# Shifted keys go straight into the candidate tile, ScalarE's copy is gone, and the engine orders, lags and PSUM banks are new

## The chip, the cores and the metric

The kernel runs on one core of one Trainium2 chip. The metric is device time in microseconds for one execution. The kernel before took 1073.24 us (median of 3 runs, 1071.86 to 1074.42). A core has five engines that run their own instruction queues side by side and meet through semaphores: TensorE (PE, with PEld for its weight loads), VectorE (DVE), ScalarE (ACT), GpSimd (POOL) and SyncE (SP, which here only issues DMAs). TensorE writes PSUM; DVE and ACT read PSUM and SBUF; POOL works on SBUF alone.

## What the reference computes

A transformer layer on 64 sequences of 64 rows of width 128. Three residual steps, each on a layer norm:

```
x = x + xattn(layernorm(x), context)   # 16 heads of 64, 128 context rows of width 96, softmax
x = x + tree(layernorm(x))             # 16 heads, depth 5: sigmoid paths, causal softmax of path agreement
x = x + experts(layernorm(x))          # product keys: 8 heads, two sets of 32 keys, top 10 of the sums
```

In the expert step each head has two score vectors of 32, s1 and s2. The reference takes the top 10 of each, adds all pairs, takes the top 10 pairs, and weighs the gelu of those pairs' hidden units by the softmax of their sums:

```
v1, i1 = top_k(s1, 10); v2, i2 = top_k(s2, 10)
vals, best = top_k(v1[:, None] + v2[None, :], 10)
h = gelu(x @ w_down[expert_idx]) * softmax(vals);  out = h @ w_up[expert_idx]
```

The kernel never gathers. It computes all 1024 hidden units (pairs of the 32 x 32 keys) for every row, forms all 1024 pair sums per head, and masks those below the cut that the top pairs set.

## The kernel before, in words

The 4096 rows are cut into 32 tiles of 128 rows (two sequences). Each tile goes through some 120 steps with names: x.* and y.* for the cross attention, t.* for the tree, k.* for the keys and their selection, e.* for the experts. Five tables (PE_ORDER, ACT_ORDER, DVE_ORDER, POOL_ORDER, SP_ORDER) hold for each engine the order of its steps in one round, and for each step a lag: in round i the engine does the step for tile i minus lag. So the engines work on several tiles at once, and each engine runs its list strictly in order; a step that waits holds all that stands behind it. A table BANK gives each result of TensorE its place in PSUM: four banks x0, x1, t0, t1 for the attention, tree and keys, and two double banks f0, f1 for the experts. A step that takes a bank waits until the last reader of its earlier content is done.

The steps around the change, for one tile:

- k.turn (PE, L528) transposes the third norm, k.high (ACT, L755) and k.low (DVE, L870) split it into two halves of 16 bits, k.key (PE, L540 and L313 to L315) makes the 512 key scores in bank t0, and e.hid (PE, L313 to L315 into psF) the 1024 hidden units.
- k.top (DVE, L944 and L947): 16 maxima of 8, then every score minus its set's maximum, written back into the same bank. k.split (DVE, L956 and L958): the shifted scores, clamped, as two 16 bit halves in the tile `us`. SP sends `us` through a transposing DMA (k.kturn) for the pair sums e.s0 to e.s7 (PE, L592).
- k.inner (POOL, L1075, L1081) writes 8 candidate sums of inner ranks into the tile `cand` of 72 per head; k.shift (ACT, L761) copies the 64 shifted scores of each head from the bank into the rest of `cand`. k.cand (DVE, L971, L976, L981) finds the best 16 of the 72.
- k.eb (ACT, L768), k.z (DVE, L989, L991) and k.lnz (ACT, L773) make the softmax's normaliser; k.cut (POOL, L1093, L1095) the cut.
- e.x (ACT, L790) exponentiates the pair sums of a head, e.w (DVE, L1002) masks them, e.a (POOL, L1123) adds the heads up. e.gelu (ACT, L780 to L782) is a table load, the gelu of the hidden units and a second table load. e.wturn, e.gate and e.out finish the tile, e.add (DVE, L1020) adds the residual.
- Around them on the same engines: x.turn (PE, L327), x.q0 to x.q3 (PE, L313 to L315 into psXT) with their copies x.w (ACT L625, one on DVE L629), the scores x.s (PE, L379), exponentials x.e (ACT, L700) and reciprocals x.r (DVE, L888), normalisation x.n (POOL, L1063), transposes x.p (PE, L398) with copies x.t (ACT, L625), the mix y.m (PE, L420, L422) with copies y.u (ACT, L625), y.out (PE, L439, L441), y.res (DVE, L899, L851 to L856), t.turn (PE, L450), t.sb (ACT, L710), t.pv (PE, L465 to L467), t.pexp and t.v (ACT, L717, L723).

Of the kernel before, what the change touches and what calls it, by code (L numbers as in the profile page):

```python
# [19 lines left out]
NQ = 2 * FH  # L20
# [9 lines left out]
def build(nc, a):  # L30
# [3 lines left out]
    with ctx:  # L34
# [229 lines left out]
        def _(pe):  # L264
# [54 lines left out]
            def x_turn(t):  # L319
                after(pe, "x.t0", t - 1)  # L320
                at_ends(pe, "x.t0", t - 2)
                at_ends(pe, "x.t0", t - 3)
                at_ends(pe, "x.t0", t - 4)
                at_ends(pe, "x.t0", t - 5)
                at_ends(pe, "x.t0", t - 6)
                pe.wait_ge(s["x.norm"], t + 1)
                done("x.turn", pe.transpose(bank[BANK["x.turn"]][:, 0:128], xn[:, t % 2, :], ident[:]))  # L327
            steps["x.turn"] = x_turn

            def queries(k):  # L330
                def step(t):
                    if k == 0:
                        after(pe, "y.res", t - 1)
                        at_ends(pe, "y.res", t - 2)
                        at_ends(pe, "y.res", t - 3)
                        at_ends(pe, "y.res", t - 4)
                        at_ends(pe, "y.res", t - 5)
                        at_ends(pe, "y.res", t - 6)
                    elif k == 1:
                        after(pe, "y.u3", t - 1)  # L340
                        at_ends(pe, "t.div", t - 2)
                        at_ends(pe, "t.div", t - 3)
                        at_ends(pe, "t.div", t - 4)
                        at_ends(pe, "t.div", t - 5)
                        at_ends(pe, "t.div", t - 6)
                        at_ends(pe, "t.div", t - 7)
                    elif k == 2:
                        pe.wait_ge(s["x.high"], t + 1)
                        pe.wait_ge(s["x.low"], t + 1)
                    elif k == 3:  # L350
                        pe.wait_ge(s["x.w2"], t + 1)
# [10 lines left out]
            def scores(k):  # L362
                def step(t):
                    if k == 0:
                        after(pe, "t.sb", t - 1)
                        at_ends(pe, "x.w1", t)
                    elif k == 1:
                        pe.wait_ge(s["x.w3"], t + 1)
                    elif k == 2:
                        pe.wait_ge(s["x.w0"], t + 1)  # L370
                    elif k == 3:
                        pe.wait_ge(s["x.e2"], t + 1)
# [12 lines left out]
            def probs_turn(k):  # L385
                def step(t):
                    if k == 0:
                        pe.wait_ge(s["y.u1"], t + 1)
                    elif k == 1:
                        pe.wait_ge(s["x.e1"], t + 1)  # L390
                    elif k == 2:
                        after(pe, "t.div", t - 1)
                        at_ends(pe, "x.e0", t)
                    elif k == 3:
                        pe.wait_ge(s["x.t2"], t + 1)
                    pe.wait_ge(s[f"x.n{k}"], t + 1)
                    for i in range(4):
                        mm = pe.transpose(bank[BANK[f"x.p{k}"]][:, i * 128:i * 128 + 128], p[:, k, i, :], ident[:])  # L398
                    done(f"x.p{k}", mm)
                return step  # L400

            def mix(k):
                def step(t):
                    if k == 0:
                        pe.wait_ge(s["y.u2"], t + 1)
                    elif k == 1:
                        pe.wait_ge(s["x.t1"], t + 1)
                    elif k == 2:
                        pe.wait_ge(s["x.e3"], t + 1)
                    elif k == 3:  # L410
                        pe.wait_ge(s["x.t3"], t + 1)
# [19 lines left out]
            def cross_out(t):  # L431
                pe.wait_ge(s["y.u0"], t + 1)
# [49 lines left out]
            def similarity(t):  # L482
                pe.wait_ge(s["t.fsb"], t + 1)
# [12 lines left out]
            def tree_mix(t):  # L496
                pe.wait_ge(s["t.exp"], t + 1)
# [15 lines left out]
            def tree_turn(t):  # L513
                pe.wait_ge(s["t.div"], t + 1)
                pe.wait_ge(s["t.div"], t + 1)
# [3 lines left out]
            def tree_out(t):  # L519
                pe.wait_ge(s["t.csb"], t + 1)  # L520
                pe.wait_ge(s["t.csb"], t + 1)
# [3 lines left out]
            def xn3_turn(t):  # L525
                pe.wait_ge(s["t.res"], t + 1)
# [4 lines left out]
            def key_scores(t):  # L531
                pe.wait_ge(s["k.high"], t + 1)
                pe.wait_ge(s["k.low"], t + 1)
# [10 lines left out]
            def hidden(t):  # L544
                after(pe, "e.w6", t - 1)
                at_ends(pe, "e.w6", t - 2)
                at_ends(pe, "e.w6", t - 3)
                at_ends(pe, "e.w6", t - 4)
                at_ends(pe, "e.w6", t - 5)
                at_ends(pe, "e.w6", t - 6)  # L550
# [11 lines left out]
            def sums(h):  # L562
                def step(t):
                    if h == 0:
                        pe.wait_ge(s["e.w2"], t + 1)
                    elif h == 1:
                        after(pe, "e.add", t - 2)
                        at_ends(pe, "e.w7", t - 1)
                        at_ends(pe, "e.add", t - 3)
                        at_ends(pe, "e.add", t - 4)  # L570
                        at_ends(pe, "e.add", t - 5)
                        at_ends(pe, "e.add", t - 6)
                        at_ends(pe, "e.add", t - 7)
                    elif h == 2:
                        pe.wait_ge(s["e.gelu"], t + 1)
                    elif h == 3:
                        pe.wait_ge(s["e.w1"], t + 1)
                    elif h == 4:
                        pe.wait_ge(s["e.w0"], t + 1)
                    elif h == 5:  # L580
                        after(pe, "e.gate", t - 1)
                        at_ends(pe, "e.w3", t)
                    elif h == 6:
                        pe.wait_ge(s["e.w4"], t + 1)
                    elif h == 7:
                        pe.wait_ge(s["e.w5"], t + 1)
# [12 lines left out]
            def w_turn(t):  # L599
                after(pe, "e.w3", t + 1)  # L600
                at_ends(pe, "e.add", t - 1)
# [7 lines left out]
            def experts_out(t):  # L609
                after(pe, "e.w7", t + 1)  # L610
                at_ends(pe, "e.gate", t)
# [52 lines left out]
        def _(act):  # L664
# [137 lines left out]
        def _(dve):  # L802
# [134 lines left out]
            def tops1(t):  # L937
# [5 lines left out]
                for k in range(NQ):  # L943
# [3 lines left out]
                done("k.top", dve.tensor_tensor(keyed, keyed, top[:, t % 2, :, 0:1].to_broadcast([128, NQ, NSQ]),  # L947
                                                ALU.subtract))
            steps["k.top"] = tops1

            def split(t):
# [3 lines left out]
                uh = bank[BANK["k.key"]].rearrange("p (h i) -> p h i", h=FH)  # L955
# [6 lines left out]
            def candidates(t):  # L962

                dve.wait_ge(s["k.shift"], t + 1)
# [251 lines left out]
```

## Time and profile before

| | |
|---|---|
| median of 3 runs | 1073.24 us (1071.86 to 1074.42) |
| span of the profiled execution (first to last instruction) | 1070.5 us |
| PE busy | 973.2 us, 91% |
| POOL busy | 893.0 us, 83% |
| ACT busy | 874.9 us, 82% |
| DVE busy | 872.4 us, 82% |
| TensorE's granted clock, mean | 0.974 of full |

The page gives one profiled execution; its own time is known as its span, which lies 2.7 us below the median of the timed runs. A busy share is an average over the span and is pulled down by the filling and the draining of the pipeline at its ends. Between them every tile looks alike, so one round can be read for all. A row of the timeline has the start in us, the time taken, the engine, the line, the operation and its tiles, and in square brackets how long the engine stood idle before it and what released it. Rows of the same line that follow each other are merged.

### The profile page before, as it was taken

The page shows a single profiled execution, that of the slowest core. Times are in us where ns is not written, and L with a number is a line of the kernel's source. Part 1 is how long each engine was busy: PE and PEld are TensorE (multiplying, and loading weights), DVE is VectorE, ACT ScalarE, POOL GpSimd, SP SyncE. Part 2 cuts the span into 40 slices and gives each one's busy share as a digit, 9 for nine tenths or more (in the row PEclk, how much of TensorE's full clock was granted, in tenths as well). Part 3 has the DMA queues.
Part 4 walks back from the last instruction along what each step waited for, and adds up shares of the span by engine and source line. Part 5 has one row for each costly group of instructions (what it writes and reads, how often), then busy time and mean ns, then how long its engine had stood idle before and what let it go on. Part 6 is the DMA issues. An engine that isn't in the chain of part 4 may idle for free.

```text
span 1070.5 us, 35810 instructions
## 1 busy us (share of the span) xinstructions
PE 973.2 (91%) x12440; PEld 763.0 (71%) x12440; DVE 872.4 (82%) x2877; ACT 874.9 (82%) x2123; POOL 893.0 (83%) x935
## 2 busy tenths in 40 slices
PE   6798999999999999999999999999999999999865
PEld 6676777777777777777777777777777777777533
DVE  3567888888888888888888888888889888888773
ACT  4668899888888988888898888889888888988752
POOL 1338888988998898889888888988888898888866
PEclk9989999999999999999999999999999999999875
DMA  6010001111110111111011111001111100110000
GB/s 168 14 23 21 18 17 27 24 27 27 23 19 16 27 24 27 27 24 23 11 26 25 27 26 27 21 11 27 25 27 26 28 20 11 27 25 21 13 13 5
DMA packets 70367, 27.25 MB, mean 25 GB/s; under 512 B 47312, under 2 KB 69936, under 8 KB 70192
## 3 DMA queue, kind: packets, MB, share of 16 engines
q1 hardware_dynamic: 69152, 24.58, 10.5%
q8 instruction: 103, 1.69, 0.7%
q14 instruction: 72, 0.59, 0.2%
q10 hardware_dynamic: 1040, 0.39, 0.1%
HBM read 14.47 MB, written 2.10 MB: 15 GB/s over the span
## 4 chain that ended last, share of the span: by engine, by line
DVE 38%; PE 29%; POOL 13%; issue 13%; ACT 6%; DVEq 1%; DMA 0%; POOLq 0%; ACTq 0%; SPq 0%
DVE mw L1002 10%; POOL wsum L1123 7%; PE psXT L398 7%; POOL p L1063 5%; PE psXT L420 5%; DVE cand L976 5%; DVE top L944 5%; PE psF L592 4%; DVE best L971 4%; DVE best L981 3%; ACT ew L790 3%; PE psXT L422 2%; DVE us L956 2%; DVE q L629 2%; DVE negmax L879 2%
## 5 line engine op out<-in xcount | busy, mean ns | idle before, releaser
L1123 POOL TENSOR_TENSOR wsum<-wsum,mw 128x1024 f32<-128x1024 f32 x192 | 452.8, 2359 | 3.1
L1002 DVE SCALAR_TENSOR_TENSOR mw<-psF,cut,ew 128x1024 f32<-128x1024 f32 x256 | 324.5, 1278 | 47.9 <-ACT ew L790 45.2
L790 ACT ACTIVATE ew<-psF,lnz 128x1024 f32<-128x1024 f32 x256 | 285.5, 1128 | 12.4 <-PE psF L592 9.3
L700 ACT ACTIVATE p<-psXT,negmax 128x128 f32<-128x128 f32 x512 | 184.0, 400 | 3.8 <-DVE negmax L879 3.7
L592 PE MATMUL psF<-sel,usT 128*128 128x512 f16 x512 | 158.5, 392 | 30.3 <-DVE mw L1002 27.7
L379 PE MATMUL psXT<-cT,q 96*128 96x128 f32 x1024 | 142.4, 282 | 14.3 <-ACT p L700 11.0
L379 PEld LDWEIGHTS psXT<-cT,q 96*128 96x128 f32 x1024 | 124.2, 191 | 43.6 <-ACT p L700 25.9
L1063 POOL TENSOR_TENSOR p<-p,rrow 128x512 f32<-128x512 f32 x128 | 130.3, 1037 | 25.9 <-DVE rrow L888 25.9
L700 ACT ACTIVATION_READ_ACCUMULATOR p<-psXT,negmax 128x1 f32 x512 | 123.9, 242 | 0.0
L420 PE MATMUL psXT<-pT,c 128*32 128x384 f32 x768 | 110.7, 501 | 2.0 <-ACT pT L625 2.0
L422 PE MATMUL psXT<-pT,c 128*32 128x128 f32 x768 | 108.5, 278 | 0.0
L313 PE MATMUL psXT<-xnT,qk 128*96 128x128 f16 x512 | 92.1, 221 | 2.2 <-DVE xnT L870 1.1
L1123 POOL TENSOR_TENSOR wsum<-mw 128x1024 f32<-128x1024 f32 x32 | 75.3, 2355 | 21.7 <-DVE mw L1002 21.7
L441 PE MATMUL psXT<-vo,uT 128*128 128x128 f32 x768 | 92.6, 277 | 0.0
L1053 POOL TENSOR_SCALAR xn<-x,mv,rstd 128x128 f32<-128x128 f32 x96 | 77.5, 808 | 17.6 <-POOL rstd L1050 17.6
L314 PE MATMUL psXT<-xnT,qk 128*96 128x128 f16 x512 | 91.9, 221 | 0.0
L315 PE MATMUL psXT<-xnT,qk 128*96 128x128 f16 x512 | 91.9, 221 | 0.0
L879 DVE TENSOR_REDUCE negmax<-psXT 128x4 f32<-128x512 f32 x128 | 85.1, 665 | 7.9 <-PE psXT L379 7.9
L441 PEld LDWEIGHTS psXT<-vo,uT 128*128 128x128 f32 x768 | 88.3, 192 | 0.0
L761 ACT ACTIVATE cand<-psXT 128x512 f32<-128x512 f32 x32 | 19.1, 597 | 83.9 <-DVE us L958 83.9
L398 PE MATMUL psXT<-ident,p 128*128 128x128 f32 x512 | 83.3, 286 | 4.2 <-POOL p L1063 0.2
L625 ACT ACTIVATE uT<-psXT 128x384 f32<-128x384 f32 x128 | 63.9, 499 | 20.0 <-PE psXT L422 20.0
(133 smaller groups left out, 2340.5 us busy)
## 6 DMA issues: line engine op xcount, KB each, us to landing
cT<-cT_dram SPq DMA_DIRECT2D x32, 96.0 KB, 2.0
c<-c_dram SPq DMA_DIRECT2D x32, 96.0 KB, 2.1
x<-x_dram SPq DMA_DIRECT2D x32, 64.0 KB, 1.8
xr<-x_dram SPq DMA_DIRECT2D x32, 64.0 KB, 2.0
y_dram<-y SPq DMA_DIRECT2D x32, 64.0 KB, 1.5
wqT<-wqT_dram SPq DMA_DIRECT2D x1, 512.0 KB, 5.1
wo<-wo_dram SPq DMA_DIRECT2D x1, 512.0 KB, 6.3
wdT<-wdT_dram SPq DMA_DIRECT2D x1, 512.0 KB, 3.5
```

Source lines behind the costliest of these rows:

```text
L379: mm = pe.matmul(bank[BANK[f"x.s{k}"]][:, i * M:i * M + M], q[:, b, h:h + 2, :].rearrange("c h q -> c (h q)"), cT[:, t % 2, b, :], start=T ...
L398: mm = pe.transpose(bank[BANK[f"x.p{k}"]][:, i * 128:i * 128 + 128], p[:, k, i, :], ident[:])
L420: pe.matmul(to[32 * j:32 * j + 32], cols, probs[:, :, 0:3, :], start=True, stop=True, tile_position=(0, 32 * j))
L422: mm = pe.matmul(to[96:128, :, j, :], cols, probs[:, :, 3, :], start=True, stop=True, tile_position=(0, 96))
L441: mm = pe.matmul(out, uT[:, i, :, :].rearrange("c b q -> c (b q)"), vo[:, i, :], start=False, stop=(i == XH3 - 1))
L592: mm = pe.matmul(bank[BANK[f"e.s{h}"]][:, j * 512:j * 512 + 512], usT[:, t % 4, h, :], sel[:, j * 512:j * 512 + 512], start=True, stop=True)
L700: ins = act.activation(p[:, k, i, :], bank[BANK[f"x.s{k}"]][:, i * M:i * M + M], ACT.Exp, bias=negmax[:, k, i:i + 1], accum_out=rowsum[:, ...
L790: done(f"e.x{h}", act.activation(ew[:, h % NEW, :], bank[BANK[f"e.s{h}"]], ACT.Exp, bias=lnz[:, t % 4, h:h + 1]))
L879: done(f"x.x{k}", dve.tensor_reduce(negmax[:, k, :], bank[BANK[f"x.s{k}"]].rearrange("p (i m) -> p i m", i=4), AX.X, ALU.max, negate=True))
L1002: done(f"e.w{h}", dve.scalar_tensor_tensor(out=mw[:, h % NMW, :], in0=bank[BANK[f"e.s{h}"]], scalar=cut[:, t % 4, h:h + 1], in1=ew[:, h % ...
L1063: done(f"x.n{k}", pool.tensor_tensor(p[:, k, :, :], p[:, k, :, :], rrow[:, k, :].unsqueeze(2).to_broadcast([128, 4, M]), ALU.mult))
L1123: done(f"e.a{h}", pool.tensor_tensor(wsum[:, t % 2, :], mw[:, 0, :] if h == 1 else wsum[:, t % 2, :], mw[:, h % NMW, :], ALU.add))
```

## The change

1. k.top's subtraction (L947) writes its result into `cand` in SBUF and no longer back into the PSUM bank.
2. k.split reads its input from `cand` and not from the bank.
3. k.shift, ScalarE's copy, is gone. k.cand waits for k.top in its place.
4. Four of the five orders are new, and so are the lags and banks. x.stats and x.norm move one tile ahead. Many waits of TensorE that other waits imply are gone, and those that the new banks ask for are new.

```
-                done("k.top", dve.tensor_tensor(keyed, keyed, top[:, t % 2, :, 0:1].to_broadcast([128, NQ, NSQ]),
-                                                ALU.subtract))
+                shifted = cand[:, t % 2, :, 0:2 * NSQ].rearrange("p h (e i) -> p h e i", e=2)
+                done("k.top", dve.tensor_tensor(shifted, keyed.rearrange("p (h e) i -> p h e i", e=2),
+                                                top[:, t % 2, :, 0:1].rearrange("p (h e) o -> p h e o", e=2)
+                                                .to_broadcast([128, FH, 2, NSQ]), ALU.subtract))
...
-                uh = bank[BANK["k.key"]].rearrange("p (h i) -> p h i", h=FH)
+                uh = cand[:, t % 2, :, 0:2 * NSQ]
...
-            def shifted(t):
-                act.wait_ge(s["k.split"], t + 1)
-                after(act, "k.cand", t - 2)
-                done("k.shift", act.activation(cand[:, t % 2, :, 0:2 * NSQ],
-                                               bank[BANK["k.key"]].rearrange("p (h i) -> p h i", h=FH), ACT.Copy))
-            steps["k.shift"] = shifted
...
-                dve.wait_ge(s["k.shift"], t + 1)
+                dve.wait_ge(s["k.top"], t + 1)
...
 PE_ORDER = {
-    "t.pv": 3, "x.s0": 2, "e.s1": 4, "x.q3": 2, "x.s2": 2, "e.s0": 4, "x.s1": 2, "t.fturn": 3, "e.s3": 4,
+    "e.hid": 4, "x.q1": 2, "e.out": 6, "t.turn": 3, "x.q0": 2, "t.pv": 3, "x.q2": 2, "e.s2": 4, "x.s0": 2,
```

The places where the order moves, as the instructions stand in a row. A lag that grows by one while the step goes from the end of a round to the start of the next changes nothing; what moves is this.

On PE, behind the key scores, before: x.turn (L327), the 24 products of e.hid (psF, first rows shown), then y.out (L439, L441), then x.q1.

```order
L327 MATMUL psXT<-ident,xn 128x128
L313 MATMUL psF<-xn3T,wd 128x128
L314 MATMUL psF<-xn3T,wd 128x128
...
L439 MATMUL psXT<-bias,ones 128x128
L441 MATMUL psXT<-vo,uT 128x128 x12
L313 MATMUL psXT<-xnT,qk 96x128
```

The same place on PE now (pair sums e.s7 at L524, y.out at L397 and L399):

```order
L524 MATMUL psF<-sel,usT 128x512 x2
L397 MATMUL psXT<-bias,ones 128x128
L399 MATMUL psXT<-vo,uT 128x128 x12
L313 MATMUL psF<-xn3T,wd 128x128
L314 MATMUL psF<-xn3T,wd 128x128
...
L313 MATMUL psXT<-xnT,qk 96x128
```

y.out has gone ahead of e.hid; e.s7, which stood ahead of k.key, now stands behind it and y.m0; x.turn has gone ahead of k.key.

On ACT, from the last copies of the mix to the exponentials of the best, before (uT is y.u, cand k.shift, gh the gelu, q x.w, xn2T t.sb, ebest k.eb, psXT L717 t.pexp, v t.v):

```order
L790 ACTIVATE ew<-psF,lnz 128x1024
L625 ACTIVATE uT<-psXT 128x6x64
L692 ACTIVATE xnT<-psXT 128x128
L761 ACTIVATE cand<-psXT 128x8x64
L780 ACT_TABLE_LOAD
L781 ACTIVATE gh<-psF 128x1024
L782 ACT_TABLE_LOAD
L625 ACTIVATE q<-psXT 96x4x2x64 x2
L710 ACTIVATE xn2T<-psXT 128x128
L625 ACTIVATE q<-psXT 96x4x2x64
L768 ACTIVATE ebest<-best 128x80
L717 ACTIVATE psXT<-psXT 128x80
```

The same place on ACT now (uT and q at L557, gh at L706, xn2T L642, v L655, psXT L649, ebest L693):

```order
L557 ACTIVATE uT<-psXT 128x6x64
L715 ACTIVATE ew<-psF,lnz 128x1024
L705 ACT_TABLE_LOAD
L706 ACTIVATE gh<-psF 128x1024
L707 ACT_TABLE_LOAD
L557 ACTIVATE q<-psXT 96x4x2x64
L642 ACTIVATE xn2T<-psXT 128x128
L557 ACTIVATE q<-psXT 96x4x2x64
L655 ACTIVATE v<-psXT 128x16x8
L649 ACTIVATE psXT<-psXT 128x80
L693 ACTIVATE ebest<-best 128x80
L557 ACTIVATE q<-psXT 96x4x2x64
```

The copy into cand is gone, so the gelu has only e.hid to wait for; t.v and t.pexp now stand ahead of k.eb, the last x.w behind it.

On DVE, from the keys' maxima to the candidates, before (L870 is x.low, mw e.w7, x and st to mv y.res):

```order
L944 MAX top<-psXT 128x8 x16
L947 TENSOR_TENSOR psXT<-psXT,top 128x512
L870 TENSOR_TENSOR xnT<-psXT,xnT 128x128
L956 TENSOR_SCALAR us<-psXT 128x8x64
L958 SCALAR_TENSOR_TENSOR us<-psXT,us 128x8x64
L1002 SCALAR_TENSOR_TENSOR mw<-psF,cut,ew 128x1024
L899 TENSOR_TENSOR x<-xr,psXT 128x128
```

The same place on DVE now (x.low at L795, k.top L869 and L873, e.w7 L929, k.split L883 and L885, y.res from L824):

```order
L795 TENSOR_TENSOR xnT<-psXT,xnT 128x128
L869 MAX top<-psXT 128x8 x16
L873 TENSOR_TENSOR cand<-psXT,top 128x8x64
L929 SCALAR_TENSOR_TENSOR mw<-psF,cut,ew 128x1024
L883 TENSOR_SCALAR us<-cand 128x8x64
L885 SCALAR_TENSOR_TENSOR us<-cand,us 128x8x64
L824 TENSOR_TENSOR x<-xr,psXT 128x128
```

x.low has gone ahead of the maxima, e.w7 between the subtraction and the split, and both instructions of the split now read cand in SBUF.

On POOL the order around this place stays k.inner, e.a5, t.norm, e.a6, k.cut; x.norm moves from behind k.norm to behind k.cut, and e.a2 from behind three of the x.n to behind two.

## Rows read from the trace of the kernel before

**Rows 1.** Timeline of SP's queue (start, took): transposing DMA of tiles 1 and 28.

```profile
100.16 1.25 SPq L226 DMA_TRANSPOSE usT<-us  x1
...
939.67 1.48 SPq L226 DMA_TRANSPOSE usT<-us  x1
```

**Rows 2.** Chain that ended last, 500 to 600 us: start, took, engine, tile, line.

```profile
562.21 1.68 DVE top L944 x16
...
573.09 0.28 ACT ebest L768
...
580.28 2.36 POOL wsum L1123
...
585.78 0.63 PE psXT L398 x4
```

**Rows 3.** Timeline of PE, one round (start, took, engine, line, operation).

```profile
561.04 0.38 PE L540 MATMUL psXT<-bias,ones 96*128 96x512 f16 x1
...
562.96 0.22 PE L313 MATMUL psF<-xn3T,wd 128*128 128x128 f16 x1
...
564.30 0.22 PE L439 MATMUL psXT<-bias,ones 96*128 96x128 f16 x1
...
567.09 0.22 PE L313 MATMUL psXT<-xnT,qk 128*96 128x128 f16 x1
...
571.37 0.27 PE L450 MATMUL psXT<-ident,xn 128*128 128x128 f32 x1
572.10 0.20 PE L465 MATMUL psXT<-bias,ones 96*128 96x80 f16 x1 [0.46 <-ACT xn2T L710]
...
572.39 0.43 PE L467 MATMUL psXT<-awv,xn2T 128*128 128x128 f32 x2
...
592.40 0.38 PE L540 MATMUL psXT<-bias,ones 96*128 96x512 f16 x1
```

**Rows 4.** Timeline of ACT, the same round.

```profile
562.95 0.49 ACT L625 ACTIVATE uT<-psXT 128x384 f32<-128x384 f32 x1 [0.50 <-PE psXT L422]
...
566.15 0.60 ACT L761 ACTIVATE cand<-psXT 128x512 f32<-128x512 f32 x1 [2.54 <-DVE us L958]
566.77 1.28 ACT L780 ACT_TABLE_LOAD   x1
...
570.40 1.08 ACT L625 ACTIVATE q<-psXT 96x512 f32<-96x512 f32 x2
571.68 0.28 ACT L710 ACTIVATE xn2T<-psXT 128x128 f32<-128x128 f32 x1 [0.20 <-PE psXT L450]
...
573.27 0.22 ACT L717 ACTIVATE psXT<-psXT 128x80 f32<-128x80 f32 x1
```

**Rows 5.** Timeline of DVE, the same round.

```profile
563.91 0.70 DVE L947 TENSOR_TENSOR psXT<-psXT,top 128x512 f32<-128x512 f32 x1
...
564.71 0.68 DVE L956 TENSOR_SCALAR us<-psXT 128x512 f16<-128x512 f32 x1
...
568.78 1.18 DVE L971 MAX8 best<-cand 128x8 f32<-128x72 f32 x8 [0.41 <-issue]
```

**Rows 6.** Page, costliest groups: busy, mean ns of one, then idle before.

```profile
L1002 DVE SCALAR_TENSOR_TENSOR mw<-psF,cut,ew 128x1024 f32<-128x1024 f32 x256 | 324.5, 1278 | 47.9 <-ACT ew L790 45.2
```

**Rows 7.** Timeline of POOL, the same round.

```profile
565.58 0.32 POOL L1075 TENSOR_TENSOR tops<-top 128x80 f32<-128x80 f32 x1
...
566.54 2.36 POOL L1123 TENSOR_TENSOR wsum<-wsum,mw 128x1024 f32<-128x1024 f32 x1
```

**Rows 8.** Timelines of DVE and POOL in the setup, about 30 us.

```profile
29.77 1.10 DVE L831 CAST wd<-wdT 128x1024 f16<-128x1024 f32 x1
...
29.27 1.04 POOL L1063 TENSOR_TENSOR p<-p,rrow 128x512 f32<-128x512 f32 x1 [5.09 <-DVE rrow L888]
30.27 1.01 POOL L1050 TENSOR_TENSOR rstd<-mv,halfneg 128x1 f32<-128x1 f32 x1
```

**Rows 9.** Line L811: duration ns min/median/max of its two forms.

```profile
L811 DVE CAST bias<-bias x2: 254/338/423, 12.4 to 40.3; 96x208 f16<-96x208 f32 x1, 96x512 f16<-96x512 f32 x1
```

More of the change, by code:

```diff
@@ L331, in step @@
                 def step(t):
[L332 to L351, printed above, removed]
                     if t == 0:
@@ L363, in step @@
                 def step(t):
[L364 to L370, printed above, removed]
+                    if k == 2:
+                        after(pe, "t.path", t - 1)
                     elif k == 3:
-                        pe.wait_ge(s["x.e2"], t + 1)
+                        after(pe, "x.e2", t)
                     pe.wait_ge(s["ld.ct"], 16 * (t + 1))
@@ L386, in step @@
                 def step(t):
[L387 to L393, printed above, removed]
+                    if k == 2:
+                        after(pe, "x.e3", t)
                     elif k == 3:
-                        pe.wait_ge(s["x.t2"], t + 1)
+                        after(pe, "t.res", t - 1)
                     pe.wait_ge(s[f"x.n{k}"], t + 1)
@@ L525, in xn3_turn @@
             def xn3_turn(t):
-                pe.wait_ge(s["t.res"], t + 1)
+                after(pe, "x.t3", t + 1)
                 pe.wait_ge(s["k.norm"], t + 1)
@@ L544, in hidden @@
             def hidden(t):
[L545 to L550, printed above, removed]
                 if t == 0:
@@ L600, in w_turn @@
                 after(pe, "e.w3", t + 1)
-                at_ends(pe, "e.add", t - 1)
+                if t >= NT - 1:
+                    after(pe, "e.add", t - 1)
                 pe.wait_ge(s[f"e.a{FH - 1}"], t + 1)
@@ L1134 @@
 PE_ORDER = {
[3 rows of a table removed]
-    "k.key": 3, "y.m0": 2, "x.turn": 1, "e.hid": 3, "y.out": 2, "x.q1": 1, "e.out": 5, "x.q0": 1, "x.q2": 1,
-    "e.s2": 3, "t.turn": 2,
[5 rows of a table added]
 }
 ACT_ORDER = {
[3 rows of a table removed]
-    2, "x.high": 1, "k.shift": 3, "e.gelu": 3, "x.w1": 1, "x.w0": 1, "t.sb": 2, "x.w2": 1,
[4 rows of a table added]
 }
 DVE_ORDER = {
-    "e.add": 6, "k.z": 4, "t.path": 3, "x.x0": 2, "e.w2": 4, "x.w3": 2, "x.x2": 2, "e.w1": 4, "e.w0": 4, "x.x1":
-    2, "x.r0": 2, "e.w3": 4, "x.r2": 2, "x.r1": 2, "x.x3": 2, "e.gate": 5, "t.div": 3, "e.w4": 4, "x.r3": 2,
-    "t.res": 3, "x.stats": 1, "e.w5": 4, "k.low": 3, "e.w6": 4, "k.top": 3, "x.low": 1, "k.split": 3, "e.w7": 4,
+    "e.add": 6, "k.z": 4, "t.path": 3, "x.x0": 2, "e.w2": 4, "x.w3": 2, "x.x2": 2, "e.w1": 4, "e.w0": 4, "x.x1": 2,
+    "x.r0": 2, "x.x3": 2, "x.r2": 2, "e.w3": 4, "x.r1": 2, "e.gate": 5, "t.div": 3, "e.w4": 4, "x.r3": 2,
+    "t.res": 3, "e.w5": 4, "e.w6": 4, "k.low": 3, "x.stats": 0, "x.low": 1, "k.top": 3, "e.w7": 4, "k.split": 3,
     "y.res": 2, "k.cand": 3,
@@ L1153 @@
 POOL_ORDER = {
-    "k.cut": 4, "t.feat": 3, "e.a7": 5, "e.a1": 4, "x.n0": 2, "x.n2": 2, "x.n1": 2, "e.a2": 4, "x.n3": 2,
-    "k.norm": 3, "x.norm": 1, "e.a3": 4, "e.a4": 4, "k.inner": 3, "e.a5": 4, "t.norm": 2, "e.a6": 4,
+    "t.feat": 3, "e.a7": 5, "e.a1": 4, "x.n2": 2, "x.n1": 2, "e.a2": 4, "x.n0": 2, "x.n3": 2, "k.norm": 3,
+    "e.a3": 4, "e.a4": 4, "k.inner": 3, "e.a5": 4, "t.norm": 2, "e.a6": 4, "k.cut": 3, "x.norm": 0,
 }
```

59 lines of the change are left out of this document (13 added, 46 removed), and 23 rows, old and new, of tables (ACT_ORDER, BANK, PE_ORDER).

## The prediction, as put on record before the run

> **What bounds the kernel now.** I read the queue of SP first, for the length of a round; then the chain of waits in the middle of the span, for what the round consists of; then the timelines of the engines over one round, for each leg of that chain. The transposing DMA comes once per tile, and from tile 1 to tile 28 it takes 939.67 - 100.16 = 839.5 us, 31.09 us per round [rows 1]. So the span is some 31 rounds and two ends, and the question is what a round becomes. In the chain the reader is to see that no single engine is the bound: it passes from DVE's maxima of the keys (562.21) over DVE's candidates to ACT's exponentials of the best (573.09), over DVE's masks to POOL's first head sum (580.28), to PE's transposes (585.78), and along PE to the key scores of the next tile [rows 2]. It is a loop through four engines, closed by one step, k.key, to which all comes back.
>
> I cut the loop at two points: the start of k.key (561.04, and 592.40 a round later [rows 3]) and the start of k.eb on ACT (573.09 [rows 2]). The first leg is 573.09 - 561.04 = 12.05 us, the second 592.40 - 573.09 = 19.31 us; together 31.36, a round that is 0.27 above the mean.
>
> The first leg has two strands beside each other. DVE's: maxima, subtraction, split, mask, y.res, candidates. ACT's: its idle 2.54 us for the split, the copy into cand (566.15), the gelu with its two table loads (566.77 to 570.40), the copies of the queries, t.sb, and then k.eb [rows 4]. Today DVE's strand ends last; ACT's is held back by the same split.
>
> **The change, part by part.**
>
> DVE's strand without its neighbours. The subtraction starts 563.91 - 561.04 = 2.87 after k.key and takes 0.70 [rows 3, 5]. From the split's first instruction to the candidates are 568.78 - 564.71 = 4.07, split, mask and y.res together [rows 5]; the order of these changes, not their content. x.low no longer stands between. The split's first instruction now reads SBUF: no row of before has it in this form; the nearest is the setup's cast from f32 to f16, SBUF to SBUF, 512 wide, 0.423 us [rows 9], against 0.68 from PSUM [rows 5]. I take 0.42, with 0.68 as the upper end, so -0.26. The second keeps two inputs of one element a step: nothing. The subtraction with its output in SBUF: nothing, since its input stays in PSUM. From the candidates' start to k.eb are 573.09 - 568.78 = 4.31. Sum: 2.87 + 0.70 + 4.07 - 0.26 + 4.31 = 11.69, that is 0.36 less than 12.05.
>
> ACT's copy. It takes 0.60 and its removal alone would let the gelu start as soon as the hidden units are there. But e.hid has been moved behind y.out, so this strand is to be summed anew. From k.key to the last copy of the mix, y.u0: 562.95 - 561.04 = 1.91, since y.m0 still follows k.key directly (x.turn moved from behind it to ahead of k.key; e.s7, now between y.m0 and y.out, lies beside y.u0). y.u0 0.49 [rows 4], and 0.14 to PE's start, as from t.sb's end (571.68 + 0.28) to t.pv at 572.10 [rows 3, 4]. y.out 567.09 - 564.30 = 2.79; e.hid 564.30 - 562.96 = 1.34, and 0.20 for the end of its last product and the hand-over to ACT (a product of 0.22 that starts 1.34 / 24 = 0.06 before y.out, and 0.04 as from t.turn's end, 571.37 + 0.27, to t.sb at 571.68) [rows 3, 4]. Here ACT stands idle, longer than the 2.54 of before. The gelu 570.40 - 566.77 = 3.63; one copy of queries, half of 1.08, is 0.54; t.sb 0.28; 0.14 to PE; t.pv 572.39 + 0.43 - 572.10 = 0.72, and 0.04 back; then t.v and t.pexp, which now stand ahead of k.eb, at the 573.27 - 573.09 = 0.18 by which such small instructions follow each other, 0.36 [rows 2 to 4]. Sum: 1.91 + 0.49 + 0.14 + 2.79 + 1.34 + 0.20 + 3.63 + 0.54 + 0.28 + 0.14 + 0.76 + 0.36 = 12.58. So the strand that took the cover of the copy is now the longer one: 0.53 more than 12.05.
>
> The second leg. POOL does the same five steps from e.a1 to the last x.n, with e.a2 one place earlier; the first transposes could start sooner, the third, which waits for the last x.n, not. On PE e.s7 (two products) leaves the stretch from there to k.key and x.turn (one) enters. On ACT, e.x6 now stands ahead of the copy x.t3, on which k.turn now waits for its bank, and y.u2 ahead of k.high; that gives back what PE gains. I cost the leg at 19.31, unchanged, with 0.3 either way. x.norm on POOL, moved behind k.cut, fills POOL's wait for t.path and costs nothing.
>
> The new contact of DVE and POOL. In the setup the only DVE instructions from SBUF to SBUF of the split's kind meet POOL at work. The 1024 wide cast at 29.77 took 1.10 us, where the two widths of L811 (0.254 for 208, 0.423 for 512) lead on to about 0.71; POOL's x.n was under way from 29.27 to 30.31, and the cast ended 0.56 after that, so it lost 0.39 of the 0.54 that they overlapped. POOL's next instruction, one element wide, took 1.01 [rows 8, 9]. So such an instruction waits behind a POOL instruction in flight, and POOL behind it. In a round POOL answers the end of the subtraction by k.inner, 566.54 - 565.58 = 0.96 us, and then the head sum e.a5, 2.36 us [rows 7]. The subtraction ends 2.87 + 0.70 = 3.57 after k.key; k.inner starts about 0.1 later (an estimate, between the hand-overs of 0.04 and 0.14 above), if POOL is idle there, which its shorter round allows; e.a5 runs from 4.63 to 6.99. DVE does the mask first, 1.28 [rows 6], and comes to the split at 4.85, just after e.a5 has started. Held to 6.85 (the cast got on about 0.14 before POOL's recorded end), it loses 2.0 us. If it wins the race instead, its second instruction, with two inputs in SBUF, meets e.a5, with much the same loss. The first leg is then 11.69 + 2.0 = 13.69, 1.64 more than before, and DVE's strand is the longer again. The stall is between nothing, where the two don't block each other, and 2.36, a whole e.a5; I take 2.0, as the one row that shows the case has nearly the full overlap lost.
>
> The Trainium skill ("SBUF — State Buffer", section "Who interferes with whom") says that a DVE instruction in a two-port mode, or with two SBUF inputs beside a GpSimd instruction that reads SBUF, and a GpSimd instruction keep each other out for the whole instruction. The setup's cast agrees but for 0.14; no row shows it for a head sum. By the rule the stall is 2.1 where the sum has 2.0. "VectorE: DVE Perf Modes", section "What auto-detection actually checks", gives such a mode to one-source instructions with both ends in SBUF, which the 0.423 of the cast bears out; the split's first instruction would be one.
>
> **The sum.** A round is 13.69 + 19.31 = 33.00, against the mean of 31.09, so 1.91 more. Of the 31 distances between 32 tiles I count 28, leaving out two while the pipeline fills and one while it drains: 28 x 1.91 = 53.5 us. The profiled span of 1070.5 lies 2.7 below the median of the runs; I add the difference to the median: 1073.2 + 53.5 = 1126.7, so 1127.
>
> **The rivals.**
>
> First: DVE and POOL do not hold each other up, or for less than the 0.9 by which ACT's strand (12.58) exceeds DVE's (11.69). Then the loop runs over y.u0, y.out, e.hid, gelu and t.pv: 12.58 + 19.31 = 31.89, 0.80 above the mean, 28 x 0.80 = 22, so 1096. For it: one short overlap in the setup is all that shows the blocking, and not beside a head sum. Against it: the 1.10 and the 1.01 of that overlap.
>
> Second, on the other side: ACT's strand is shorter than I read, because PE gets to e.hid sooner. If e.hid ends 0.89 earlier than in my sum, and the split is not held, DVE's strand alone counts: 11.69 + 19.31 = 31.00; and the 0.36 by which this leg shrinks would come off the mean round too: 31.09 - 0.36 = 30.73, up to 0.1 less with PE's stretch shorter. 28 x 0.45 = 12.6, so 1061. It decides from the point at which ACT's strand falls below 12.05 - 0.27 = 11.78. For it: PE stands idle in the round (0.46 ahead of t.pv [rows 3]), and e.s7 has moved. Against it: y.out can't start ahead of y.u0, and each term is from a row.
>
> Third: gains and losses cancel, 1073, with ACT's strand near 11.8 and a stall under 0.2.
>
> **How the numbers follow.** A stall that ends last 0.47, ACT's strand 0.26, faster 0.19, no change 0.08. The likeliest gives 1127; with its stall between 1.3 and 2.36 and the second leg 0.3 either way, 28 x (1.2 to 2.3) gives 1107 to 1137 for it alone. The range for 8 in 10 runs from 1062 to 1137: it takes in the stall of nothing (1096), no change, and about half of the faster case. Within 0.2% (2 us) a measurement of this kernel can't tell from no change. Faster 0.19, same 0.08, slower 0.73.
>
> **What would show it.** In the profile of the changed kernel: the transposing DMAs 33.0 apart. The split's first instruction with a recorded time well above 0.42, near 2.4 if its wait is inside, or the second one likewise, each time beside e.a5; or else e.a5 longer than 2.36. k.eb 13.7 after k.key's start, waiting for DVE's candidates. If k.eb is 12.6 after k.key and DVE waits for ACT there, with ACT idle over 3 us for e.hid, the first rival holds. If the split's first instruction takes 0.42 beside e.a5, with k.eb under 11.8 after k.key, I am wrong in both steps. If the second leg is off 19.31 by over 0.5, my reading of PE's and ACT's new order there is wrong.

## The result, and the profile after

The changed kernel took 1128.32 us (median of 4 runs, 1126.6 to 1132.16), the kernel before beside it 1073.5 (1071.86 to 1074.42): ratio 1.0516 [1.0501, 1.0532], slower, 1.3 us above the forecast of 1127. The span of its profiled execution is 1126.8 us, 56.3 more than before. The medians of the kernel before beside the experiments lie between 1072.9 and 1074.4.

SP's queue of the changed kernel gives the length of a round, as [rows 1] did (start, took):

```profile
70.45 1.37 SPq L226 DMA_TRANSPOSE usT<-us  x1
108.96 1.25 SPq L226 DMA_TRANSPOSE usT<-us  x1
...
990.24 1.24 SPq L226 DMA_TRANSPOSE usT<-us  x1
```

The last two are of tiles 1 and 28: 881.28 / 27 = 32.64 us a round, 1.55 more than before; 27 of these are 41.8 us. The other 14.5 are at the ends: the first transpose comes 2.6 later than before (67.81 there), the distance to the second is 38.51 instead of 32.35, and from tile 28 to the end of the span are 136.6 instead of 130.8.

Inside a round, PE's timeline of the changed kernel (start, took, engine, line, operation) to be held against [rows 3]: k.key, y.out, e.hid, the next k.key.

```profile
589.99 0.38 PE L482 MATMUL psXT<-bias,ones 96*128 96x512 f16 x1
...
592.44 0.23 PE L397 MATMUL psXT<-bias,ones 96*128 96x128 f16 x1
...
595.24 0.22 PE L313 MATMUL psF<-xn3T,wd 128*128 128x128 f16 x1
...
622.53 0.38 PE L482 MATMUL psXT<-bias,ones 96*128 96x512 f16 x1
```

ACT's timeline of the same round, for [rows 4], with the idle time ahead in brackets: the last mix copy, the gelu's table load, t.pexp, k.eb.

```profile
591.89 0.49 ACT L557 ACTIVATE uT<-psXT 128x384 f32<-128x384 f32 x1 [1.33 <-PE psXT L381]
...
596.85 1.28 ACT L705 ACT_TABLE_LOAD   x1 [3.35 <-PE psF L315]
...
602.38 0.23 ACT L649 ACTIVATE psXT<-psXT 128x80 f32<-128x80 f32 x1
603.30 0.27 ACT L693 ACTIVATE ebest<-best 128x80 f32<-128x80 f32 x1 [0.69 <-DVE best L908]
```

The first leg is 603.30 - 589.99 = 13.31 us (12.05 in the round of before that was read), the second 622.53 - 603.30 = 19.23 (19.31). All that a round lost lies in the first. By the median over the rounds that start with the k.key of tiles 2 to 26 the two legs are 11.70 and 19.30 in the kernel before, 13.31 and 19.24 now: the round of before that was read is longer than most, and the part on the prediction comes back to it. ScalarE now waits 3.35 for e.hid, its strand is done at 602.61, 12.62 after k.key, and k.eb still stands idle 0.69 for DVE. So DVE ends last, and its timeline, for [rows 5 and 6], shows by what:

```profile
592.85 0.69 DVE L873 TENSOR_TENSOR cand<-psXT,top 128x512 f32<-128x512 f32 x1
593.53 1.28 DVE L929 SCALAR_TENSOR_TENSOR mw<-psF,cut,ew 128x1024 f32<-128x1024 f32 x1
594.73 2.50 DVE L883 TENSOR_SCALAR us<-cand 128x512 f16<-128x512 f32 x1
597.26 0.69 DVE L885 SCALAR_TENSOR_TENSOR us<-cand,us 128x512 f16<-128x512 f32 x1
...
599.00 1.18 DVE L898 MAX8 best<-cand 128x8 f32<-128x72 f32 x8
```

POOL's timeline beside it, for [rows 7]:

```profile
593.61 0.32 POOL L1002 TENSOR_TENSOR tops<-top 128x80 f32<-128x80 f32 x1 [0.59 <-DVE cand L873]
594.01 0.61 POOL L1008 TENSOR_TENSOR cand<-tops 128x32 f32<-128x32 f32 x3
594.58 2.36 POOL L1050 TENSOR_TENSOR wsum<-wsum,mw 128x1024 f32<-128x1024 f32 x1
599.03 0.56 POOL L977 TENSOR_TENSOR rstd<-mv,halfneg 128x1 f32<-128x1 f32 x1 [2.09 <-DVE mv L781]
```

The mask (L929) has its old 1.28. The split's first instruction starts 0.15 after POOL's head sum e.a5 and is recorded as busy for 2.50; e.a5 keeps its 2.36 and pays nothing. Then POOL itself stands idle 2.09, for y.res, which is queued on DVE behind the held split. The groups of the split's two lines (duration in ns, minimum, median, maximum) say that this is the rule and not one round:

```profile
L883 DVE TENSOR_SCALAR us<-cand x32: 426/2490/2574, 69.2 to 1084.8; 128x512 f16<-128x512 f32 x32
...
L885 DVE SCALAR_TENSOR_TENSOR us<-cand,us x32: 691/693/2708, 69.7 to 1087.3; 128x512 f16<-128x512 f32 x32
```

The 426 is tile 0, which comes before any head sum. The 2708 is the last tile, where two head sums follow each other on POOL and the second instruction of the split is held as well as the first.

A held instruction looks like a busy one. The page's first part has DVE busy for 66.7 us more (872.4 before), though its list of work has hardly changed:

```profile
PE 982.7 (87%) x12440; PEld 768.1 (68%) x12440; DVE 939.1 (83%) x2877; ACT 859.7 (76%) x2091; POOL 895.4 (79%) x935
```

The groups by line (busy time, mean ns, idle ahead) put 58 us of these on the split, whose two lines were 21.8 and 22.1 us before:

```profile
L883 DVE TENSOR_SCALAR us<-cand 128x512 f16<-128x512 f32 x32 | 77.8, 2432 | 0.0
...
L885 DVE SCALAR_TENSOR_TENSOR us<-cand,us 128x512 f16<-128x512 f32 x32 | 24.2, 756 | 1.1
```

The pipeline's filling, in the view by stretches (length, busy time of PE, PEld, DVE, ACT, POOL, then PE's granted clock), first the kernel before, from its first transpose to its second:

```profile
67.81:100.16 32.35, 28.33 (x364) 21.49 (x363) 24.37 (x87) 27.25 (x67) 20.87 (x27) 0.95 0.09 21
```

and the same stretch of the changed kernel:

```profile
70.45:108.96 38.51, 33.21 (x404) 26.72 (x402) 27.74 (x88) 27.99 (x66) 23.70 (x30) 0.87 0.07 17
```

While few tiles are under way each wait leaves PE idle, and here its clock was granted at 0.87 where before it had 0.95. This stretch alone cost 6.2 us.

### The profile page after: what moved, and what is told of

Read it like the earlier page. It is cut to its first block, busy times and chain, and to the rows that moved or that the text cites. A ratio compares the mean times of both kernels' runs of the same rounds, so it can differ in the third digit from the quotient of the medians.

```text
span 1126.8 us, 35109 instructions
## 1 busy us (share of the span) xinstructions
PE 982.7 (87%) x12440; PEld 768.1 (68%) x12440; DVE 939.1 (83%) x2877; ACT 859.7 (76%) x2091; POOL 895.4 (79%) x935
## 4 chain that ended last, share of the span: by engine, by line
DVE 32%; POOL 21%; PE 21%; issue 14%; ACT 11%; DVEq 1%; DMA 0%; POOLq 0%; ACTq 0%; SPq 0%
POOL wsum L1050 12%; POOL p L990 9%; DVE us L883 7%; ACT ew L715 6%; DVE mw L929 6%; PE psXT L379 5%; DVE cand L903 5%; PE psXT L363 4%; DVE best L898 3%; DVE best L908 3%; PE psF L524 2%; PE psXT L381 2%; ACT p L632 2%; DVE q L561 2%; DVE negmax L804 1%
## 5 line engine op out<-in xcount | busy, mean ns | idle before, releaser
L929 DVE SCALAR_TENSOR_TENSOR mw<-psF,cut,ew 128x1024 f32<-128x1024 f32 x256 | 324.5, 1279 | 16.3 <-ACT ew L715 14.1
L524 PE MATMUL psF<-sel,usT 128*128 128x512 f16 x512 | 160.5, 396 | 36.4 <-DVE mw L929 27.9
L349 PEld LDWEIGHTS psXT<-cT,q 96*128 96x128 f32 x1024 | 127.9, 193 | 48.1 <-ACT p L632 25.9
L977 POOL TENSOR_TENSOR rstd<-mv,halfneg 128x1 f32<-128x1 f32 x96 | 54.6, 569 | 92.2 <-DVE mv L781 92.2
L705 ACT ACT_TABLE_LOAD x32 | 41.1, 1283 | 106.0 <-PE psF L315 106.0
L313 PE MATMUL psXT<-xnT,qk 128*96 128x128 f16 x512 | 94.6, 222 | 1.8 <-DVE xnT L795 1.8
L314 PE MATMUL psXT<-xnT,qk 128*96 128x128 f16 x512 | 94.6, 222 | 0.0
L315 PE MATMUL psXT<-xnT,qk 128*96 128x128 f16 x512 | 94.5, 222 | 0.0
L399 PE MATMUL psXT<-vo,uT 128*128 128x128 f32 x768 | 92.7, 277 | 0.0
L557 ACT ACTIVATE uT<-psXT 128x384 f32<-128x384 f32 x128 | 60.1, 506 | 42.4 <-PE psXT L381 42.2
L399 PEld LDWEIGHTS psXT<-vo,uT 128*128 128x128 f32 x768 | 88.6, 192 | 0.0
```

What stands on the lines that cost most here:

```text
L349: mm = pe.matmul(bank[BANK[f"x.s{k}"]][:, i * M:i * M + M], q[:, b, h:h + 2, :].rearrange("c h q -> c (h q)"), cT[:, t % 2, b, :], start=T ...
L399: mm = pe.matmul(out, uT[:, i, :, :].rearrange("c b q -> c (b q)"), vo[:, i, :], start=False, stop=(i == XH3 - 1))
L524: mm = pe.matmul(bank[BANK[f"e.s{h}"]][:, j * 512:j * 512 + 512], usT[:, t % 4, h, :], sel[:, j * 512:j * 512 + 512], start=True, stop=True)
L929: done(f"e.w{h}", dve.scalar_tensor_tensor(out=mw[:, h % NMW, :], in0=bank[BANK[f"e.s{h}"]], scalar=cut[:, t % 4, h:h + 1], in1=ew[:, h % ...
```

## The experiments

My theory: the split, now reading SBUF, is held by POOL's head sum; beside it the new orders let the gelu wait for e.hid behind y.out. The rivals are that the orders alone cost it all, or that the data flow alone does. Rounds below are the mean distance of the transposes of tiles 1 to 28.

**1. The orders alone.** New orders, old flow: the subtraction back into the bank, the split from the bank, ScalarE's copy.

```
-                shifted = cand[...]; dve.tensor_tensor(shifted, ...)        # k.top
+                dve.tensor_tensor(keyed, keyed, ...)
-                uh = cand[:, t % 2, :, 0:2 * NSQ]
+                uh = bank[BANK["k.key"]].rearrange(...)
-  ... "e.x7": 4, "e.gelu": 3
+  ... "e.x7": 4, "k.shift": 3, "e.gelu": 3
```

Expected: 

> The new orders, lags and banks with the old flow of data: subtraction in place in PSUM, split from PSUM, ScalarE's copy put back ahead of the gelu. Theory (split held by POOL's head sum on top of a longer ScalarE strand): the hold is gone, the first leg falls back to ScalarE's strand (k.key to k.eb 12.6 us, read in the changed kernel), the round is 12.6 + 19.2 = 31.8, and the filling stays 9 us longer: 28 x 0.75 + 9 = 30 us over before, 1103 us. Rival 1 (the orders cost everything): 1128 us. Rival 2 (the flow of data costs everything): 1073 us.

Measured: 1096.41 us, ratio 1.0202 [1.0183, 1.0222], a round of 31.70. The split from PSUM is not held (its first instruction, all 32 of them):

```profile
L888 DVE TENSOR_SCALAR us<-psXT x32: 678/681/691, 69.4 to 1056.1; 128x512 f16<-128x512 f32 x32
```

So of the 55 us of loss, 32 need the new flow, and 23 come with the new orders around the old flow; run 9 comes back to the 23.

**2. The flow alone.** The kernel before with the three edits of the flow and its own orders.

```
-                dve.tensor_tensor(keyed, keyed, ...)                         # k.top
+                shifted = cand[...]; dve.tensor_tensor(shifted, ...)
-                dve.wait_ge(s["k.shift"], t + 1)                             # k.cand
+                dve.wait_ge(s["k.top"], t + 1)
-  "k.shift": 3, "e.gelu": 3
+  "e.gelu": 3
```

Expected: 

> The old orders with the new flow of data: subtraction into the candidates, split from SBUF, no copy on ScalarE. Theory: the split now follows the subtraction directly, while POOL is still in the head sum e.a4 for about 0.9 us, and its second instruction may meet k.inner's small ones: the split loses 0.6 to 1.0 us net and the round grows by that, 28 x 0.8 = 22 us, 1095 us; the split's first instruction is recorded near 1.2 us, not 2.5. Rival (no hold, or none that matters): the first leg shrinks by 0.26, 1066 to 1073 us.

Measured: 1087.52 us, ratio 1.0129 [1.0114, 1.0144], a round of 31.57. The flow alone loses too, but less than it does among the new orders, and 7.5 us less than the 1095 that was expected. The split's first instruction is held here as well, for less:

```profile
L951 DVE TENSOR_SCALAR us<-cand x32: 427/1211/1280, 68.5 to 1046.9; 128x512 f16<-128x512 f32 x32
```

That is the 1.2 that was expected. POOL's timeline shows the reason: at 573.75, when the split starts, the pair of head sums ahead of k.inner is in its last 0.9 us, and the split, with its 0.42, gets through behind it.

```profile
569.88 4.80 POOL L1118 TENSOR_TENSOR wsum<-wsum,mw 128x1024 f32<-128x1024 f32 x2
574.63 0.50 POOL L1070 TENSOR_TENSOR tops<-top 128x80 f32<-128x80 f32 x1
575.22 0.95 POOL L1076 TENSOR_TENSOR cand<-tops 128x32 f32<-128x32 f32 x3
```

Then it is POOL's turn to be held: its small instructions take 0.50 where they took 0.32 [rows 7], and 0.95 where the changed kernel has 0.61. Where the split stands against the head sums decides what it loses: 0.79 here, 2.07 behind the mask.

**3. The head sum out of the way.** The changed kernel with e.a5 behind t.norm on POOL.

```
-    "k.inner": 3, "e.a5": 4, "t.norm": 2,
+    "k.inner": 3, "t.norm": 2, "e.a5": 4,
```

Expected: 

> The changed kernel with one step moved: on POOL the head sum e.a5 stands behind t.norm and not ahead of it, so POOL has nothing to do while the split runs. Theory: the split's first instruction falls from 2.49 to 0.42 us, k.eb then waits for ScalarE's strand at 12.6 after k.key, the round is 31.8, 1103 us. Rival (the hold is not what bounds the round): 1128 us, or more, since POOL now idles for 2.5 us more per round.

Measured: 1105.72 us, ratio 1.0304 [1.0269, 1.0338], a round of 31.97. The hold is gone; in DVE's timeline the split takes 0.42, and the normaliser now waits for ScalarE's k.eb:

```profile
585.71 0.42 DVE L883 TENSOR_SCALAR us<-cand 128x512 f16<-128x512 f32 x1
...
593.66 0.24 DVE L916 TENSOR_REDUCE z<-ebest 128x8 f32<-128x80 f32 x1 [1.29 <-ACT ebest L693]
```

The first leg is 593.37 - 580.97 = 12.40, ScalarE's strand, 0.18 below the 12.58 of my sum. Same operations, same operands, other neighbour, and 0.417 by the median of all 32: this shows the hold directly. The part of the loss that remains is for the next runs.

**4. e.hid ahead of y.out.** The changed kernel with the gelu's input early, as before.

```
-    "e.hid": 4, "x.q1": 2, ...     "e.s7": 4, "y.out": 2,
+    "x.q1": 2, ...                 "e.s7": 4, "e.hid": 3, "y.out": 2,
```

Expected: 

> The changed kernel with e.hid back ahead of y.out on TensorE. It shortens ScalarE's strand by about 2.8 us and leaves the hold. Theory: VectorE's strand with the hold still ends last, the round stays 32.6, only the filling gets shorter by up to 6 us: 1121 to 1128 us. Rival (ScalarE's strand bounds the round): the round falls by 0.7, 1106 us.

Measured: 1128.9 us, ratio 1.0512 [1.0497, 1.0528], a round of 32.70: nothing gained. It is just above the expected 1121 to 1128, since the filling got shorter by 1.1 and not by up to 6 (the first two transposes are 37.37 apart). ACT's timeline shows the gelu's wait down from 3.35 to 0.29, and the time standing in a later wait instead, ahead of t.sb and of k.eb:

```profile
560.51 1.28 ACT L705 ACT_TABLE_LOAD   x1 [0.29 <-PE psF L315]
...
567.70 0.28 ACT L642 ACTIVATE xn2T<-psXT 128x128 f32<-128x128 f32 x1 [2.97 <-PE psXT L406]
...
570.02 0.27 ACT L693 ACTIVATE ebest<-best 128x80 f32<-128x80 f32 x1 [0.69 <-DVE best L908]
```

So the 106.0 us that ScalarE idles for e.hid in the changed kernel, the longest wait in its profile, cost next to nothing while DVE is held.

**5. The subtraction twice.** The changed kernel, with the shifted keys written to SBUF for the candidates and also back into PSUM, from where the split reads; no copy on ScalarE.

```
                 dve.tensor_tensor(shifted, ...)
+                done("k.top", dve.tensor_tensor(keyed, keyed, ..., ALU.subtract))
...
-                uh = cand[:, t % 2, :, 0:2 * NSQ]
+                uh = bank[BANK["k.key"]].rearrange(...)
```

Expected: 

> The changed kernel with the subtraction done twice on VectorE, once into the candidates and once in place in PSUM, and the split reading PSUM again; the order is the same and POOL's head sum still starts beside the split. It adds 0.6 us to VectorE's strand and takes the contact away. Theory (the hold is a matter of the split reading SBUF): the split takes 0.68 and 0.69 us, VectorE's strand is about 12.1, below ScalarE's 12.4, and the round is that of the kernel with e.a5 moved, 31.9: 1103 us. Rival (the hold comes from another use of POOL or of the order): the split stays near 2.5 us and the time goes to 1128 us or above, as VectorE has more to do.

Measured: 1096.26 us, ratio 1.0213 [1.0196, 1.0231], a round of 31.72. The split is not held; its first instruction, all 32 of them:

```profile
L885 DVE TENSOR_SCALAR us<-psXT x32: 677/680/692, 70.5 to 1055.7; 128x512 f16<-128x512 f32 x32
```

In the round from 575.67 on it starts at 580.93, 0.06 behind POOL's head sum, and takes 0.68. One more DVE instruction of 0.69 per tile, and 32 us faster than the changed kernel: the cost is not in the amount of DVE's work. The leg is 12.40 there, and k.z waits for ScalarE's k.eb, so ScalarE's strand ends last, as in run 3; the 1103 that was expected from run 3 missed the second leg, which is 19.25 here and 19.52 in run 3, with POOL's step moved.

**6. Only the second instruction of the split from SBUF.** As 5, with `in0=uc` (the candidates in SBUF) in the second instruction alone.

Expected: 

> As the kernel with two subtractions, but only the split's first instruction reads PSUM; its second reads the candidates and its own first result, two inputs in SBUF, while POOL's e.a5 is in flight. If two inputs in SBUF are held like the one-input form at two elements a step, the second instruction is recorded near 2.0 to 2.5 us (0.69 without a hold) and the time is near 1120 us; if only the form at two elements a step is held, 0.69 and about 1103 us.

Measured, one run: 1131.06 us, a round of 32.77. The second instruction, two inputs in SBUF (0.69 in every kernel where it is not held), is held like the first:

```profile
L888 DVE SCALAR_TENSOR_TENSOR us<-cand,us x32: 698/2134/2140, 69.9 to 1089.5; 128x512 f16<-128x512 f32 x32
```

So had the first won the race against e.a5, the second would have been held, as the prediction said. The Trainium skill ("SBUF — State Buffer", section "Who interferes with whom") names both kinds, a DVE instruction in a two-port mode and one with two SBUF inputs, the latter beside a GpSimd instruction that reads SBUF; the changed kernel and this run agree, with 2.07 and 1.44 us lost to one head sum.

**7. Both repairs, 3 and 4, together.**

Expected: 

> The changed kernel with both steps moved: e.a5 behind t.norm on POOL (no hold) and e.hid ahead of y.out on TensorE (shorter ScalarE strand). Theory (two strands, the longer one sets the first leg): neither alone brings it down to before, both together do: y.out now ends later and y.res waits for it, k.eb about 12.0 after k.key, the round 31.3, the filling some 7 us longer than before: 1085 us. Rival (a third bound in the new orders): 1100 us or above.

Measured: 1134.45 us, ratio 1.0569 [1.0548, 1.059], a round of 32.99: my expectation missed by 50 us, on the wrong side. The first leg is as I said (573.39 - 561.42 = 11.97), but the second became 594.06 - 573.39 = 20.67. POOL's timeline:

```profile
569.11 0.56 POOL L977 TENSOR_TENSOR rstd<-mv,halfneg 128x1 f32<-128x1 f32 x1 [3.04 <-DVE mv L781]
...
570.62 4.79 POOL L1050 TENSOR_TENSOR wsum<-wsum,mw 128x1024 f32<-128x1024 f32 x2
575.37 0.19 POOL L1020 TENSOR_TENSOR cut<-best 128x8 f32<-128x8 f32 x1
...
582.24 2.36 POOL L1050 TENSOR_TENSOR wsum<-mw 128x1024 f32<-128x1024 f32 x1
```

e.a5 had filled POOL's wait for y.res. Moved behind t.norm, it leaves POOL idle 3.04 there, since e.hid ahead of y.out makes y.res late too; k.cut then comes right behind two head sums, and e.a1, with which the second leg begins, starts at 582.24, about 1.4 after its mask is done. I had counted two strands in the first leg, but POOL is a third: its list of one round fits only while nothing of it waits.

**8. A try on the kernel before: k.key ahead of e.s7** on PE.

```
-    "e.s7": 4, "k.key": 3,
+    "k.key": 3, "e.s7": 4,
```

Expected: 

> The kernel before with one pair swapped on TensorE: k.key goes ahead of e.s7, as the new orders have it; all else is the old kernel. If the loop through k.key is what sets the round, k.key comes 0.3 us sooner (then k.low holds it), the second leg falls from 19.3 to 19.0, and the time by 28 x 0.3 = 8 us, 1065 us. Rival (e.s7 being later holds the last exponential and mask, and with them VectorE's strand): 1074 us or more.

Measured: 1078.18 us, ratio 1.0043 [1.0028, 1.0058], a round of 31.20: a miss, the rival was right. In the list of waits (total, times, longest) the kernel before has

```profile
ACT ew L790 <- PE psF L592: 9.3, 8, 3.5
```

and this one

```profile
ACT ew L790 <- PE psF L592: 36.1, 37, 3.4
```

The pair sums that gave way are the next input of ScalarE's exponentials, and these stand on ACT ahead of the strand that should have gained. The second leg did fall to 19.00 by the median of the rounds, as expected, but the first grew from 11.70 to 12.12.

**9. The orders alone (1), with e.hid ahead of y.out.**

Expected: 

> The new orders with the old flow (subtraction back into PSUM, split from PSUM, ScalarE's copy), and e.hid put ahead of y.out again on TensorE. The new orders with the old flow took 1096 us with a round of 31.70. Theory: what was left of that loss is ScalarE's strand, gelu late behind y.out; with e.hid first the gelu starts as early as before, the round comes down to 31.1 to 31.3 and the time to 1080 to 1085 us (27 rounds of 0.4 to 0.6 less; the longer filling stays). Rival: another strand is as long (POOL, whose t.norm waits for y.res, now later), and the time stays at 1092 to 1100 us.

Measured: 1094.92 us, ratio 1.02 [1.0175, 1.0226], a round of 31.65. The theory missed. It was not e.hid: in the old flow ScalarE's copy waits for the split, which in the new orders stands behind the mask, and the gelu is queued behind the copy. ACT's timeline:

```profile
548.56 0.60 ACT L693 ACTIVATE cand<-psXT 128x512 f32<-128x512 f32 x1 [2.67 <-DVE us L890]
```

So most of the 23 us of run 1 belong to the old flow among orders that were made for the new one (run 11 moves only this copy and is 14 us faster); they are not a part of the changed kernel's loss that can be added to the hold.

**10. The subtraction twice (5), with e.hid ahead of y.out.**

Expected: 

> The changed kernel with the subtraction done twice, into SBUF for the candidates and back into PSUM for the split, and e.hid put ahead of y.out. With the second subtraction alone it took 1096 us, a round of 31.72. Theory: no hold, no copy on ScalarE, gelu early: the round is set by VectorE's strand, 12.05 with 0.70 for the second subtraction and without 0.3 for x.low, so a round near 31.3 to 31.5 and 1083 to 1091 us. Rival: POOL's wait for the later y.res sets the round, as with both edits together, and the time stays at 1096 us or goes above it.

Measured: 1084.9 us, ratio 1.0117 [1.01, 1.0134], a round of 31.33, within the expectation. With neither copy nor hold, e.hid's place is worth 11 us. In the round from 534.79 on the first leg is 12.01 (k.key at 534.79, k.eb at 546.80) and the second 19.25.

**11. The copy beside the mask.** The orders of 9; ScalarE's copy waits for the subtraction, the split for the copy.

```
-                act.wait_ge(s["k.split"], t + 1)      # k.shift
+                act.wait_ge(s["k.top"], t + 1)
...
+                dve.wait_ge(s["k.shift"], t + 1)      # k.split
```

Expected: 

> The new orders with the subtraction back into PSUM and e.hid ahead of y.out, and ScalarE's copy now waits for the subtraction instead of the split, the split for the copy; so the copy (0.60) lies beside VectorE's mask e.w7 (1.28) and VectorE has one subtraction only. Theory: the doubled subtraction with e.hid first had a round of 31.26 in which VectorE stood still nowhere from its maxima to its candidates, with ScalarE 1.6 us ahead; 0.6 less on VectorE gives 30.6 to 30.8, and the time 1063 to 1071 us, under the kernel before. Rival: the copy comes too late behind e.x7 and holds the split, or POOL sets the round, which stays at 31.2 or more: 1078 to 1086 us.

Measured: 1080.64 us, ratio 1.0071 [1.0057, 1.0084], a round of 31.31: a miss, and in the rival's range, though for another reason than the rival's. The copy does lie beside the mask, and DVE is through the split 0.5 sooner after k.key than in 10, but then (DVE's timeline)

```profile
540.62 0.69 DVE L891 SCALAR_TENSOR_TENSOR us<-psXT,us 128x512 f16<-128x512 f32 x1
541.69 0.29 DVE L831 TENSOR_TENSOR x<-xr,psXT 128x128 f32<-128x128 f32 x1 [0.37 <-PE psXT L399]
```

y.res waits for y.out, which stands behind e.hid. The leg is 547.13 - 535.16 = 11.97, 0.04 less than in 10. This is the fastest kernel with the new orders; none tried here beat the kernel before.

## Why the prediction was right

**The hold.** The term "2.0 us behind e.a5" measured 2.50 - 0.42 = 2.08 in the round shown, 2.49 - 0.42 = 2.07 by the median. The place, the instruction, the race (DVE 0.15 behind e.a5) and the freed point (DVE went on 0.13 before POOL's recorded end, as the 0.14 of the setup [rows 8]) are as predicted. Runs 3 and 5 show it as the cause: without the overlap the same instruction takes 0.42, and a split from PSUM beside e.a5 takes 0.68.

**DVE's strand.** Without the hold it is 13.31 - 2.07 = 11.24, against 11.69. The difference is a term that should not have been in the sum: the pause of 0.41 ahead of the candidates (marked "issue" in the last of [rows 5]), which the 4.07 takes in. The list of waits of the kernel before (total, times, longest) has it once in all 32 tiles:

```profile
DVE best L971 <- issue: 0.4, 1, 0.4
```

The tile of that one pause is the one whose round was read. Without it the sum is 11.28. The split from SBUF takes the 0.42 that I read off a cast [rows 9].

**ScalarE's strand.** Predicted 12.58 to k.eb; done at 12.62 in the changed kernel, and where it ends last, in run 3, k.eb comes after 12.40. It lay under the longer one, as predicted, and run 4 shows that it cost next to nothing there. The rival built on it, 31.89 a round and 1096, is near what run 5 measured, 31.72 and 1096.26; that the totals agree so closely is luck, as run 5 has a smaller round and more at the ends.

**The second leg.** 19.23 for 19.31. What PE, ACT and POOL exchange there does cancel.

**The count of rounds.** Here a size was off, and the total hides it. The round grew by 1.55 and not by 1.91, which is 41.8 over 27 rounds instead of 53.5 over 28. The 1.91 sets 33.00, built on a round with a pause, against a mean of 31.09. Not every tile looks alike: seven of the 25 rounds of tiles 2 to 26 are 0.2 to 0.4 longer than the 31.01 of the median, by pauses whose cause is not shown, and the round that was read is among the longest, with 31.36. A typical one has k.key at 498.68 and k.eb, on ACT, 11.70 later:

```profile
510.38 0.27 ACT L768 ACTIVATE ebest<-best 128x80 f32<-128x80 f32 x1 [0.30 <-DVE best L981]
```

Without the pause the sum is 11.28 + 2.0 + 19.31 = 32.59, 1.58 above 31.01; the changed kernel's median round is 32.55. The other error is that I let the ends cost nothing, where they cost 14.5. The two errors, 11.7 and 14.5, nearly cancel, so it is luck that the total came out within 1.3 us, while the hold itself was forecast to 0.1. The filling pays more than a round does: its first distance grew by 6.2, at a lower clock. Of the 38.51, e.hid early takes 1.1 off by itself (37.37, run 4), a split from PSUM without the copy 4.4 (34.10, run 5), and both together bring it to 32.7 (run 10), near the 32.35 of before. Where the hold is taken away by POOL's other order, 36.52 (run 3) and 35.31 (run 7) remain, so the filling depends on the other steps' places too; that was not followed further.

**The gain that was not there.** Taking a copy of 0.60 off ScalarE had nothing to give by itself: before the change ScalarE's strand did not end last. The best round found among the new orders without the hold (31.3 in the mean of run 11) is not under the 31.09 of the kernel before, since y.res waits for y.out as soon as DVE is 0.5 faster.

## What to carry to other kernels

Before a sum is built on one round, compare that round with its neighbours: here the one that was read had a pause of 0.41 that a typical one does not have. Before moving an operand from PSUM to SBUF to save a copy, look at what POOL runs at the moment when the new SBUF reader is due: here 0.26 us gained on the instruction and 0.60 on another engine were paid with 2.07. A hold is not shown as a wait; look for one form of instruction whose median is far above its minimum, and then at POOL's row at that time. In a loop that closes through four engines, repair one thing at a time and measure: two repairs that each were neutral or better (3 and 4) were together the slowest kernel of all.

## What the runs showed of the hardware that was not expected

- The hold is one-sided when POOL is first: e.a5 kept 2.36 us while DVE lost 2.07. When DVE is first, POOL's small instructions pay: 0.32 became 0.50 and 0.61 became 0.95 (run 2).
- An instruction with an f32 input in SBUF and one f16 input in SBUF, which runs at the same 0.69 as with its first input in PSUM, is held too (2.13 us, run 6). Reading at the lower pace does not protect it.
